# Graph network with skip LSTMs: the LSTM input read in dense runs, the end state transposed in fp32

## The chip, the cores and the metric

The kernel runs on one core of a Trainium2 chip. The metric is the device time of one execution in microseconds (us), the median of repeated runs; lower is better.

## The reference

Eight batch elements of 1,024 nodes with 128 features pass through two graph networks, each followed by a residual sum and a layernorm. The second network ends in four LSTMs over windows of consecutive nodes, one for each window length p = 1, 2, 3, 4; each replaces the last node of its windows, and the next p reads the result. Cut to what matters here:

```python
def _lstm_last(Wih, Whh, bih, bhh, xs):            # xs [windows, p, 128]
    def step(carry, x_t):
        h, c = carry
        g = x_t @ Wih.T + h @ Whh.T + bias
        i, f, gg, o = jnp.split(g, 4, axis=-1)
        c = jax.nn.sigmoid(f) * c + jax.nn.sigmoid(i) * jnp.tanh(gg)
        h = jax.nn.sigmoid(o) * jnp.tanh(c)
        return ((h, c), None)
...
h = jax.nn.relu(jnp.einsum('ts,bsh->bth', adj, x @ Wg0 + bg0))
h = jax.nn.relu(jnp.einsum('ts,bsh->bth', adj, h @ Wg1 + bg1))
for p in range(1, MAX_SKIP + 1):
    nw = Tv // p
    wins = h[:, :nw * p, :].reshape(Bv * nw, p, Hd)
    last = _lstm_last(Wih[p - 1], Whh[p - 1], bih[p - 1], bhh[p - 1], wins)
    idx = jnp.arange(nw) * p + (p - 1)
    h = h.at[:, idx, :].set(last.reshape(Bv, nw, Hd))
...
x = _layernorm(x + _L0_gnn_ref(x, adj, adj, ...), axis=-1)
x = _layernorm(x + _L1_gnn_ref(x, adj, ...), axis=-1)
```

## The kernel before

Everything stays in SBUF, features or nodes on the 128 partitions. Each fp32 product is made of three matmuls of rounded parts (fp32r): high by high, high by low, low by high. `product` issues the three, and its lines L464, L465 and L466 carry nearly all matmuls. ScalarE rounds a result to its high part, VectorE subtracts for the low part (`lo_part`, L916), and only then can the next product read it.

The first network runs in four pairs of batch elements and ends near 547 us. Then come nine slots (0 to 8). A slot works on several batch elements at once: the graph products of element n (`adj_x`, `wg0`, `adj_h`, `wg1`), the LSTM of p = 1 and 2 for element n-1 and of p = 3 and 4 for element n-2. The text calls a window length "span p". Slots 3 to 6 are two turns of a loop over two slots. The orders are written out by hand in the lists `SLOT` (slots 0 to 6), `DRAIN` (slot 7) and `LAST` (slot 8), and all engines follow the same list. An item `step(stream, p, s, ...)` is step s of span p. Spans 1 and 2 run in stream Y, 3 and 4 in X, and element 7 in Z. `("ahead",)` lets TensorE do the input products of the following step early. `held=True` lets the end of a step on ScalarE and VectorE come after the next step's gates. `("fin", v, back)` brings the end state back to nodes on partitions, four tiles of 128 nodes for each v, and adds it to `xb`; `stats`, `root` and `scale` are the layernorm on VectorE.

A step has 3 gates (s = 0) or 4. The gates' input products come first, 3 matmuls for each gate; at s > 0 as many recurrent products on `hstep` follow. That makes, for one batch element, 9 + 12 = 21 input matmuls for span 2, 33 for span 3 and 45 for span 4. After the gates ScalarE applies the functions (L861), VectorE multiplies (L1167 to L1174), ScalarE takes tanh (L871), and VectorE multiplies once more (L1186), casts the high part (L1188) and subtracts the low part (L916).

The state of an element lies in `ht`, features on partitions, nodes in their order along the free axis, in a high and a low part, two elements in turn (`ht_last` for element 7). The input of step s of span p is every p-th column:

```python
first = u.w0 * u.p + u.s
return slice(first, first + u.p * (nw - 1) + 1, u.p)
```

So TensorE's moving operand has a step of 2, 3 or 4 fp32 elements, and the last step of a span writes its state back with that step. `fin` multiplies `ht`, high and low, by an identity: 8 fp32r matmuls for each v (L754, L755), 16 for each element.

Of the kernel before, what the change touches and what calls it, by code (L numbers as in the profile page):

```python
# [8 lines left out]
F32 = mybir.dt.float32  # L29
# [5 lines left out]
P = 128  # L35
# [7 lines left out]
GI, GF, GG, GO = range(4)  # L43


def build(nc, x, adj_t, w1, w2, w3, wg0, bg0, wg1, bg1, wih_t, whh_t, bih, bhh, out):
# [10 lines left out]
    with ctx:  # L57
# [19 lines left out]
        xb = sb("xb", [P, B, MT, F], F32)  # L77
# [14 lines left out]
        HTW = N + 2  # L92
# [9 lines left out]

        ht = sb("ht", [P, 2, 2, HTW], F32R, r3_at)
        gates_at = (r3_at + 4 * 4 * HTW + 63) // 64 * 64
        gates = sb("gates", [P, 2, 5, BANK], F32, gates_at)
        hstep = sb("hstep", [P, 2, 2, BANK], F32R, gates_at + 4 * 10 * BANK)

        ht_last = sb("ht_last", [P, 2, HTW], F32R, adj_at)
        gates_last = sb("gates_last", [P, 5, BANK], F32, adj_at + 12 * KB)
        hstep_last = sb("hstep_last", [P, 2, BANK], F32R, adj_at + 12 * KB + 4 * 5 * BANK)  # L110
        assert gates_at + 4 * 14 * BANK <= lw_raw_at + 4 * (2 * SKIPS - 1) * G4 + 64
# [10 lines left out]
        ident = sb("ident", [P, P], F32R)  # L122
# [44 lines left out]
        h_done = sem("h_done")  # L167
        fin_mm = sem("fin_mm")
# [48 lines left out]
        Step = namedtuple("Step", "stream p s w0 nw n back held")  # L217
        X, Y, Z = 0, 1, 2

        def step(stream, p, s, w0=0, back=None, nw=None, held=False):  # L220
            nw = nw or min(N // p, BANK)
            return Step(stream, p, s, w0, nw, nw + nw % 2, (2 if stream == X else 1) if back is None else back,
                        held)
# [85 lines left out]
        CELL_STEPS = (2, 4)  # L309
# [6 lines left out]
            "cell": lambda n: sum(CELL_STEPS[u.s > 0] for u in steps_of(n)),  # L316
# [9 lines left out]
        FIN_PRE = 2  # L326
# [44 lines left out]
        def span(u, n=None):  # L371

            at = u.w0 % BANK
            return slice(at, at + (n or u.n))

        def h_in(slot, back):

            return ht_last if slot - back == B - 1 else ht[:, :, (slot - back) % 2, :]

        def gates_in(stream):  # L380
            return gates_last if stream == Z else gates[:, stream]

        def hstep_in(stream):
            return hstep_last if stream == Z else hstep[:, :, stream]
# [7 lines left out]
        def columns(u, nw):  # L392

            first = u.w0 * u.p + u.s
            return slice(first, first + u.p * (nw - 1) + 1, u.p)
# [905 lines left out]
```

## Time and profile before

| what | value |
|---|---|
| time, median of 3 runs (lowest, highest) | 1154.91 us (1154.67, 1155.43) |
| the profiled execution's own time, beside its span | span 1154.9 us, which is its time from the first to the last instruction |
| TensorE busy | 1121.8 us (97%) |
| VectorE busy | 583.2 us (50%) |
| ScalarE busy | 386.3 us (33%) |
| GpSimd busy | 0.7 us |
| mean granted TensorE clock | 0.989 of full |

TensorE's busy time counts from a matmul's start to the end of its drain, and matmuls overlap. A matmul's price in a stream is the distance from its start to the start of the next one; its own duration is longer.

### The profile page before, as it was taken

What the parts mean: (1) busy time and instruction counts of PE and PEld (TensorE: products, weight loads), DVE (VectorE), ACT (ScalarE), POOL (GpSimd) and SP (SyncE); (2) the same over time, 40 slices, a digit from 0 to 9 for tenths busy, and PEclk for the clock granted to TensorE, in tenths of its full rate; (3) what the DMA queues carried; (4) which work ended last, traced back from release to release, by engine and by line L of the source; (5) the groups of instructions that cost most, each with busy time, mean ns of one, the idle gap of its engine ahead of it and who ended that gap; (6) DMA issues with size and microseconds to landing.
All of it is one profiled execution on the core that took longest, in us unless ns stands there. A gap on an engine that the chain in (4) does not pass through costs nothing.

```text
span 1154.9 us, 15131 instructions
## 1 busy us (share of the span) xinstructions
PE 1121.8 (97%) x5688; PEld 937.5 (81%) x5688; DVE 583.2 (50%) x1426; ACT 386.3 (33%) x696; POOL 0.7 (0%) x6
## 2 busy tenths in 40 slices
PE   6999999999999999999999999999999999999994
PEld 4888988899888988888776878878788787778694
DVE  7233364243442264247646545565655646565667
ACT  6222012120222012133424443444434443435442
POOL 0000000000000000000000000000000000000000
PEclk9999999999999999999999999999999999999997
DMA  9200000000000000012000000000000000000001
GB/s 312 85 1 1 1 1 1 1 1 1 0 0 0 0 0 0 0 39 106 1 1 1 1 1 1 1 19 1 19 1 0 18 0 2 17 19 1 1 19 37
DMA packets 21744, 20.43 MB, mean 18 GB/s; under 512 B 960, under 2 KB 18496, under 8 KB 21696
## 3 DMA queue, kind: packets, MB, share of 16 engines
q1 hardware_dynamic: 21696, 19.81, 5.4%
q8 instruction: 28, 0.46, 0.2%
q14 instruction: 20, 0.16, 0.0%
HBM read 15.61 MB, written 4.19 MB: 17 GB/s over the span
## 4 chain that ended last, share of the span: by engine, by line
PE 94%; DVE 3%; ACT 1%; DMA 0%; issue 0%; ACTq 0%; SPq 0%; DVEq 0%
PE ps L464 27%; PE ps L465 27%; PE ps L466 27%; PE ps L584 8%; PE ps L563 4%; PE ps L566 1%; DVE adj L916 1%; PE ps L755 1%; PE ps L754 0%; DMA xb<-in_x 0%; PE ps L600 0%; DVE square L982 0%; DVE stats L933 0%; DVE node L916 0%; DVE xb L974 0%
## 5 line engine op out<-in xcount | busy, mean ns | idle before, releaser
L861 ACT ACTIVATE gates<-ps,lb 128x256 f32<-128x256 f32 (+2 forms) x273 | 142.6, 567 | 168.1 <-PE ps L466 155.1
L464 PE MATMUL ps<-adj,node 128*128 128x512 f32 x384 | 151.9, 396 | 12.8 <-DVE adj L916 10.1
L465 PE MATMUL ps<-adj,node 128*128 128x512 f32 x384 | 150.3, 391 | 0.0
L466 PE MATMUL ps<-adj,node 128*128 128x512 f32 x384 | 150.3, 391 | 0.0
L801 ACT ACTIVATE y<-ps 128x512 fp32r<-128x512 f32 x48 | 28.7, 598 | 294.5 <-PE ps L466 294.4
L916 DVE TENSOR_TENSOR y<-ps,y 128x512 fp32r<-128x512 f32 x48 | 33.1, 691 | 186.0 <-ACT y L801 186.0
L466 PE MATMUL ps<-ht,lw 128*128 128x256 f32 (+2 forms) x231 | 112.1, 485 | 0.0
L465 PE MATMUL ps<-ht,lw 128*128 128x256 f32 (+2 forms) x231 | 111.9, 485 | 0.0
L464 PE MATMUL ps<-ht,lw 128*128 128x256 f32 (+2 forms) x231 | 111.0, 480 | 0.0
L464 PE MATMUL ps<-adj,h 128*128 128x512 f32 x256 | 99.7, 389 | 0.0
L465 PE MATMUL ps<-adj,h 128*128 128x512 f32 x256 | 99.7, 389 | 0.0
L466 PE MATMUL ps<-adj,h 128*128 128x512 f32 x256 | 99.6, 389 | 0.0
L464 PEld LDWEIGHTS ps<-adj,node 128*128 128x128 f32 x384 | 73.0, 190 | 28.7 <-DVE adj L916 10.8
L919 DVE SCALAR_TENSOR_TENSOR h<-ps,h 128x512 fp32r<-128x512 f32 x112 | 76.5, 690 | 35.2 <-ACT h L801 34.4
L584 PE MATMUL ps<-s,adj 128*128 128x256 f32 x768 | 93.0, 283 | 0.0
L584 PEld LDWEIGHTS ps<-s,adj 128*128 128x128 f32 x768 | 92.4, 192 | 0.0
L466 PEld LDWEIGHTS ps<-adj,node 128*128 128x128 f32 x384 | 72.5, 189 | 15.7
L465 PEld LDWEIGHTS ps<-adj,node 128*128 128x128 f32 x384 | 72.9, 190 | 14.7
L801 ACT ACTIVATE h<-ps 128x512 fp32r<-128x512 f32 x96 | 57.4, 598 | 48.9 <-PE ps L466 46.1
L466 PEld LDWEIGHTS ps<-ht,lw 128*128 128x128 f32 x231 | 48.0, 208 | 22.2 <-issue 12.2
L1186 DVE TENSOR_TENSOR gates<-gates 128x256 f32<-128x256 f32 (+3 forms) x77 | 42.0, 546 | 39.7 <-ACT gates L871 39.7
L464 PEld LDWEIGHTS ps<-ht,lw 128*128 128x128 f32 x231 | 46.9, 203 | 18.3 <-issue 7.7
(167 smaller groups left out, 1975.5 us busy)
## 6 DMA issues: line engine op xcount, KB each, us to landing
square<-in_adj_t SPq DMA_DIRECT2D x8, 512.0 KB, 8.0
xb<-in_x SPq DMA_DIRECT2D x8, 512.0 KB, 7.5
adj_raw<-in_adj_t SPq DMA_DIRECT2D x8, 512.0 KB, 7.7
out<-xb SPq DMA_DIRECT2D x7, 512.0 KB, 3.2
lw_raw<-in_wih_t SPq DMA_DIRECT2D x1, 1024.0 KB, 5.8
lw_raw<-in_whh_t SPq DMA_DIRECT2D x1, 768.0 KB, 7.3
w_raw<-in_w SPq DMA_DIRECT2D x1, 512.0 KB, 11.0
out<-xb SPq DMA_DIRECT2D x2, 256.0 KB, 2.5
```

Of the source, the lines that this page charges most:

```text
L464: pe.matmul(dst, stat(HI), mov(HI), start=start, stop=False)
L465: pe.matmul(dst, stat(HI), mov(LO), start=False, stop=False)
L466: return pe.matmul(dst, stat(LO), mov(HI), start=False, stop=stop)
L563: pe.matmul(ps[:, q % BANKS, 2 * t * F:(2 * t + 2) * F], h2[:, HI, k, nt:nt + P], w3s[:, k, :, :].rearrange("p a c -> p (a c)"), start=(k ...
L566: last = pe.matmul(ps[:, q % BANKS, 2 * t * F:(2 * t + 1) * F], h2[:, LO, k, nt:nt + P], w3s[:, k, HI, :], start=False, stop=(k == K3 - 1) ...
L584: last = pe.matmul(dst, adj[:, a, m, nt:nt + P], s3[:, b, m, :, :].rearrange("p j c -> p (j c)"), start=(m == 0 and t == 0 and (a, b) == ( ...
L755: last = pe.matmul(dst, h_in(slot, back)[:, LO, nt:nt + P], ident[:], start=False, stop=True)
L801: nc.scalar.activation(dst, ps[:, (j * A_MM + q) % BANKS, :], func).then_inc(a_hi, 1)
L861: nc.scalar.activation(gates_in(u.stream)[:, g, at], ps[:, (AHEAD["gate"][slot] + gate) % GB, 0:u.n], ACT.Tanh if g == GG else ACT.Sigmoid ...
L916: nc.vector.tensor_tensor(dst, src, f32(hi), ALU.subtract).then_inc(done, 1)
L919: nc.vector.scalar_tensor_tensor(out=dst, in0=src, scalar=0.0, in1=f32(hi), op0=ALU.max, op1=ALU.subtract).then_inc(done, 1)
L1186: nc.vector.tensor_tensor(h, h, in_place(v, GG, n), ALU.mult).then_inc(cell_step, 1)
```

## The change

The nodes are put in another order outside the kernel: node i goes to place (i % 4) * 256 + i // 4, four groups of 256 (x, and both sides of the adjacency matrix; the output is put back). In that order the input of span 2 is two runs of 256 adjacent columns. For spans 3 and 4 the state is kept a second time, in `hw`: twelve runs of 86 columns, run r holding the nodes with i % 12 = r, at a pitch of 88. Span 3 reads 4 runs for a step (344 columns where there were 342), span 4 reads 3 (258 where there were 256).

The even runs (the nodes that p = 2 leaves as they are) are copied from `ht` by GpSimd, one copy for the high and one for the low part of each element, after p = 1 and after step 2 of span 4 of the element before. The odd runs are written by VectorE as the end of span 2, and span 3 writes its four runs. The end state of span 3 is summed (high + low) to plain fp32 in `hfull` for three of the four groups; the last step of span 4 writes the fourth group there in one multiply, without a high and a low part. `fin` takes 4 fp32 transposes for each v out of `hfull` instead of 8 fp32r matmuls. `ht` has one buffer instead of two, the streams' `gates` and `hstep` are separate tensors, and the lists of items stay as they are.

```diff
+def node_order(n):
+    return np.arange(n).reshape(n // BLOCKS, BLOCKS).T.reshape(n)
...
+        def inputs_of(u, slot, i):
+            if u.p == 1:
+                return h0[:, i, u.w0:u.w0 + u.n]
+            if u.p == 2:
+                return h_in(slot, u.back)[:, i, :].rearrange("q (w s u) -> q s w u", w=2, s=2)[:, u.s]
+            return runs_in(slot, u.back)[:, i, :].rearrange("q (w s v) -> q s w v", s=u.p, v=PITCH)[:, u.s, :, 0:RUN]
...
+            back = 1
+            for slot in range(back, SLOTS):
+                steps = steps_of(slot)
+                ready = max(k for k, u in enumerate(steps) if u.p == 1 and u.back == back)
+                if slot - back < B - 2:
+                    ready = max([ready] + [k for k, u in enumerate(steps) if (u.p, u.s) == (4, 2)])
+                if slot - back == B - 2:
+                    pool.wait_ge(out_done, 16 * OUT_BEFORE_LATE)
+                pool.wait_ge(h_done, AHEAD["unit"][slot] + ready + 1)
+                of, to = h_in(slot, back), runs_in(slot, back)
+                for i in (HI, LO):
+                    last = nc.gpsimd.tensor_copy(half_of_runs(to[:, i, :], 0), f32(spread(of, i * N, [[N // 2, 2]])))
+                last.then_inc(runs_set, 1)
...
+                        if (u.p, u.s) == (3, 0):
+                            pe.wait_ge(runs_set, batch_of(slot, turn, u.back) + 1)
...
                         for t in range(4):
-                            nt = (4 * v + t) * P
-                            dst = mm_unit(v)[:, t * F:(t + 1) * F]
-                            pe.matmul(dst, h_in(slot, back)[:, HI, nt:nt + P], ident[:], start=True, stop=False)
-                            last = pe.matmul(dst, h_in(slot, back)[:, LO, nt:nt + P], ident[:],
-                                             start=False, stop=True)
+                            at = (2 * v + t // 2) * OPEN_BLOCK + t % 2 * P
+                            last = pe.transpose(mm_unit(v)[:, t * F:(t + 1) * F], full_in(slot, back)[:, at:at + P],
+                                                ident_f[:])
...
+                            if ends(v):
+                                block = full_in(slot, v.back)[:, (BLOCKS - 1) * OPEN_BLOCK:]
+                                nc.vector.tensor_tensor(
+                                    block.rearrange("q (v a) -> q a v", a=PER_BLOCK),
+                                    h.rearrange("q (a v) -> q a v", a=PER_BLOCK),
+                                    tanh.rearrange("q (a v) -> q a v", a=PER_BLOCK), ALU.mult).then_inc(h_done, 1)
+                                continue
...
+                            if (v.p, v.s) == (3, 2):
+                                dve.wait_ge(h_done, ahead("unit", slot, turn, n_ended))
+                                hi, lo = (f32(runs_in(slot, v.back)[:, i, :]).rearrange(
+                                    "q (a b v) -> q b a v", a=PER_BLOCK, v=PITCH)[:, 0:BLOCKS - 1, :, 0:RUN]
+                                    for i in (HI, LO))
+                                nc.vector.tensor_tensor(full_in(slot, v.back)[:].rearrange(
+                                    "q (b v a) -> q b a v", b=BLOCKS, a=PER_BLOCK)[:, 0:BLOCKS - 1], hi, lo, ALU.add)
```

On VectorE, in the second half of a slot, these rows of before stand between the last step of span 4 (`gates`, 256 wide, the first row) and the layernorm's `scale` (the last row); the 512-wide rows are step 0 of span 2:

```order
560 L1186 TENSOR_TENSOR gates<-gates 128x256
561 L1153 REGISTER_ALU
562 L1188 CAST ht<-gates 128x256
563 L1153 REGISTER_ALU
564 L916 TENSOR_TENSOR ht<-gates,ht 128x256
565 L1184 REGISTER_ALU
566 L1186 TENSOR_TENSOR gates<-gates 128x512
567 L1153 REGISTER_ALU
568 L1188 CAST hstep<-gates 128x512
569 L1153 REGISTER_ALU
570 L916 TENSOR_TENSOR hstep<-gates,hstep 128x512
```

In the change the same place reads (`gates_x` is stream X's, `hfull` the fp32 end state):

```order
559 L1224 TENSOR_TENSOR hfull<-gates_x 128x3x86
560 L1218 REGISTER_ALU
561 L1229 TENSOR_TENSOR gates<-gates 128x512
562 L1194 REGISTER_ALU
563 L1246 CAST hstep<-gates 128x512
564 L1194 REGISTER_ALU
565 L966 TENSOR_TENSOR hstep<-gates,hstep 128x512
```

Two instructions of the end of span 4 are gone. At the end of span 3 VectorE has one more in the change, behind the cast and the low part, and ahead of the low part of `z`:

```order
471 L1229 TENSOR_TENSOR gates_x<-gates_x 128x344
472 L1194 REGISTER_ALU
473 L1246 CAST hw<-gates_x 128x4x86
474 L1194 REGISTER_ALU
475 L966 TENSOR_TENSOR hw<-gates_x,hw 128x4x86
476 L1256 TENSOR_TENSOR hfull<-hw 128x3x3x86
477 L1186 REGISTER_ALU
478 L966 TENSOR_TENSOR z<-ps,z 128x512
```

The row with `hfull<-hw` (774 columns) is the added one. GpSimd had only its constants and the identity; now it has two copies for each of the eight elements:

```order
6 L492 MEMSET ident_f 128x128
7 L494 ISA
8 L494 AFFINE_SELECT ident_f<-ident_f 128x128
9 L508 CAST hw<-ht 128x2x3x86 x12
10 L508 CAST hw_late<-ht 128x2x3x86 x2
11 L508 CAST hw_last<-ht_last 128x2x3x86 x2
```

The last three rows are new, 516 columns each.

## Rows read from the trace of the kernel before

**Rows 1.** The page: busy time, the 40 slices, and one costly group.
```profile
PE 1121.8 (97%) x5688; PEld 937.5 (81%) x5688; DVE 583.2 (50%) x1426; ACT 386.3 (33%) x696; POOL 0.7 (0%) x6
...
PE   6999999999999999999999999999999999999994
...
L464 PE MATMUL ps<-ht,lw 128*128 128x256 f32 (+2 forms) x231 | 111.0, 480 | 0.0
```

**Rows 2.** Busy by window: about one slot of the loop (us and count per engine).
```profile
698.00:771.00 73.00, 73.00 (x334) 58.08 (x333) 42.76 (x108) 31.09 (x59) 0.00 (x0) 1.00 0.03 8
```

**Rows 3.** Timeline of TensorE, slot 5: first matmul of each block (start, us).
```profile
698.89 0.46 PE L464 MATMUL ps<-ht,lw 128*128 128x342 f32 x1
701.60 0.43 PE L464 MATMUL ps<-adj,node 128*128 128x512 f32 x1
...
710.69 0.34 PE L464 MATMUL ps<-hstep,lw 128*128 128x342 f32 x1
...
712.60 0.22 PE L464 MATMUL ps<-wgs,z 128*128 128x128 f32 x1
...
745.28 0.39 PE L464 MATMUL ps<-ht,lw 128*128 128x256 f32 x1
...
748.06 0.30 PE L464 MATMUL ps<-hstep,lw 128*128 128x256 f32 x1
...
749.49 0.61 PE L464 MATMUL ps<-ht,lw 128*128 128x512 f32 x1
...
753.59 0.42 PE L464 MATMUL ps<-z,wgs 128*128 128x512 f32 x1
...
754.55 0.61 PE L464 MATMUL ps<-ht,lw 128*128 128x512 f32 x1
...
760.00 0.24 PE L754 MATMUL ps<-ident,ht 128*128 128x128 f32 x1
...
760.87 0.45 PE L464 MATMUL ps<-hstep,lw 128*128 128x512 f32 x1
...
763.69 0.22 PE L754 MATMUL ps<-ident,ht 128*128 128x128 f32 x1
...
772.07 0.46 PE L464 MATMUL ps<-ht,lw 128*128 128x342 f32 x1
```

**Rows 4.** Timeline of VectorE, slot 5: a dense and a stepped cast, two ends.
```profile
745.17 0.29 DVE L1188 CAST hstep<-gates 128x256 fp32r<-128x256 f32 x1
...
755.30 0.40 DVE L1188 CAST ht<-gates 128x256 fp32r<-128x256 f32 x1
...
757.44 0.69 DVE L916 TENSOR_TENSOR hstep<-gates,hstep 128x512 fp32r<-128x512 f32 x1
```

**Rows 5.** Lines of GpSimd: mean ns after the busy us.
```profile
L456 POOL TENSOR_SCALAR_AFFINE_SELECT ident_f<-ident_f 128x128 f32<-128x128 f32 x1 | 0.3, 294 | 0.1
L454 POOL MEMSET ident_f<- 128x128 f32 x1 | 0.2, 205 | 0.3 <-POOLq L1291 0.3
```

**Rows 6.** Timeline of VectorE in slot 1, behind step 0 of span 2.
```profile
612.27 4.19 DVE L974 TENSOR_SCALAR xb<-xb,mv,newton 128x128 f32<-128x128 f32 x16
616.38 0.68 DVE L919 SCALAR_TENSOR_TENSOR h<-ps,h 128x512 fp32r<-128x512 f32 x1
```

**Rows 7.** Timeline of TensorE, slot 8: its start and two waits.
```profile
1049.79 0.39 PE L464 MATMUL ps<-h,lw 128*128 128x512 f32 x1
...
1090.99 0.55 PE L464 MATMUL ps<-ht_last,lw 128*128 128x342 f32 x1 [2.15 <-DVE ht_last L916]
...
1136.23 0.49 PE L464 MATMUL ps<-hstep_last,lw 128*128 128x256 f32 x1 [1.65 <-DVE hstep_last L916]
```

**Rows 8.** Busy by window, with granted clock (the 1.00 or 0.57).
```profile
1091.00:1099.00 8.00, 8.00 (x29) 7.73 (x30) 5.98 (x23) 2.02 (x4) 0.00 (x0) 0.57 0.00 0
```

**Rows 9.** Timeline of VectorE: the end of the last step of all.
```profile
1140.79 0.39 DVE L1188 CAST ht_last<-gates_last 128x256 fp32r<-128x256 f32 x1
1141.22 0.61 DVE L916 TENSOR_TENSOR ht_last<-gates_last,ht_last 128x256 fp32r<-128x256 f32 x1
```

More of the change, by code:

```diff
@@ L307, in count, with ends, cell_steps @@
             return sum(item[0] == name for item in items(slot) if not isinstance(item, Step))
-        CELL_STEPS = (2, 4)
+        def ends(u):
+            return u.p == SKIPS and u.s == SKIPS - 1
+        def cell_steps(u):
+            return (2 if u.s > 0 else 0) + (0 if ends(u) else 2)
         PER_SLOT = {
@@ L369, in needs, with span, runs_in, full_in @@
             return before(slot, k, lambda v, b: b + v.back == u.back and (v.p, v.s) == (u.p - 1, u.p - 2))
-        def span(u, n=None):
-            at = u.w0 % BANK
-            return slice(at, at + (n or u.n))
+        def span(u):
+            return slice(0, u.n)
         def h_in(slot, back):
-            return ht_last if slot - back == B - 1 else ht[:, :, (slot - back) % 2, :]
+            return ht_last if slot - back == B - 1 else ht
+        def runs_in(slot, back):
+            return hw_last if slot - back == B - 1 else hw_late if slot - back == B - 2 else hw
+        def full_in(slot, back):
+            return hfull_last if slot - back == B - 1 else hfull_late if slot - back == B - 2 else hfull
         def gates_in(stream):
-            return gates_last if stream == Z else gates[:, stream]
+            return (gates_x, gates, gates_last)[stream]
         def hstep_in(stream):
-            return hstep_last if stream == Z else hstep[:, :, stream]
+            return (hstep_x, hstep, hstep_last)[stream]
         def place_before(slot, k):
@@ L616, in bank_free @@
                         pe.wait_ge(a_lo, A_PRE + PAIRS * A_LO_PAIR)
-                    elif slot >= 2:
-                        pe.wait_ge(fin_add, ahead("fin", slot, turn, FIN_PRE + r - 1))
+                    elif slot >= 3:
+                        pe.wait_ge(fin_add, ahead("fin", slot, turn, r - 1))
                 def mm_unit(r):
@@ L1245, in dve_slot @@
                         if item[0] == "stats":
-                            dve.wait_ge(fin_add, ahead("fin", slot, turn, FIN_PRE + n_fin))
+                            dve.wait_ge(fin_add, ahead("fin", slot, turn, n_fin))
                             group_stats(groups, at)
@@ L1250, in dve_slot @@
                             v = item[1]
-                            dve.wait_ge(fin_add, ahead("fin", slot, turn, FIN_PRE + n_fin))
+                            dve.wait_ge(fin_add, ahead("fin", slot, turn, n_fin))
                             last = row_stats(groups[4 * v:4 * v + 4])
```

129 lines of the change are left out of this document (77 added, 52 removed).

## The prediction

> **What bounds the kernel now.** I read the page first: TensorE is busy for 97% of the span, and its row of tenths shows 9 in nearly every slice; VectorE has 50%, ScalarE 33%, GpSimd nothing [rows 1]. Then the windows: in 73 us of the loop TensorE is busy all the time at full clock, VectorE for 42.8 us and ScalarE for 31.1 [rows 2]. Busy time alone doesn't prove a full TensorE, since matmuls overlap, so the third view is the timeline, where the distance from one block to the next is what a block costs [rows 3]. A slot of the loop is 772.07 - 698.89 = 73.18 us. The reader should compare four pairs there. 9 input products of span 2 take 753.59 - 749.49 = 4.10 us and 12 take 5.45, so 0.455 each; 12 recurrent products of the same 512 columns, from dense `hstep`, take 763.69 - 760.87 = 2.82, so 0.235. For span 3, 9 input products take 2.71, 0.301 each, and 12 dense ones of 342 columns take 1.91, 0.159 each. For span 4, 12 take 2.78, 0.232 each, and 12 dense ones 1.43, 0.119 each. Same engine, clock and width; only the step of the moving operand differs, and a step of 2, 3 or 4 elements costs the same factor, 1.9 to 2. TensorE bounds the loop, and 99 matmuls of each element (231 x 3 plus those on `ht_last`, 792 in all [rows 1]) are read at half rate.
>
> **What each part is worth.** Input products, for one element:
> - span 2: 21 x (0.455 - 0.232) = 4.7 us. I take 0.232 for a dense one; 0.235 is the row, and stationary loads alike.
> - span 3: 33 x (0.301 - 0.160) = 4.65 us. The 2 extra columns of 344 are in the 0.160.
> - span 4: 45 x (0.232 - 0.120) = 5.0 us.
>
> Together 14.4 us, if runs of 86 and 256 columns are read like one dense stretch. The trace has no moving operand in several runs. The bounds are the dense rows (14.4) and the stepped rows for spans 3 and 4 (4.7 only). I take the dense ones: 85 of 86 steps inside a run are steps to the neighbour.
>
> `fin`: 8 matmuls of 128 columns take 760.87 - 760.00 = 0.87 us, 0.109 each, 1.7 us for an element [rows 3]. The change has 8 fp32 transposes instead of 16. No row has one. Below, it costs what one fp32r matmul costs, 0.109, and an element gains 0.85 us. Above, full fp32 is done as four passes of parts: 0.44 each, 3.5 us, a loss of 1.8. I take the lower end, since a transpose multiplies nothing and the kernel's own three-part product exists for the sake of multiplying.
>
> The Trainium skill speaks on both sides: "TensorE: Matmul & The Clock Gate", Terms, says that the transpose mode is four times faster for fp32, and "FP8 and Floating Point Precision", TensorE Precision Notes, that true fp32 takes four passes. No row here decides it.
>
> VectorE: the end of span 4 loses a cast and a low part, 0.40 and some 0.6 us; span 3 gains an addition of 774 columns, about 1.0 us by 0.69 for 512 [rows 4]. Even in sum. The stepped cast took 0.40 where a dense one of the same size took 0.29, so the stepped reads at the end of span 2 may add up to 0.5 us for an element. All of that lies under TensorE in the loop, and costs its full length where TensorE waits for a state.
>
> GpSimd: two copies of 516 columns for each element. Its only rows of size are 128 columns in 0.205 and 0.294 us [rows 5], which scale to 0.83 and 1.19; with the 40% that a step cost VectorE up to 1.7. So 1.7 to 3.4 us for both. They may start when step 2 of span 4 is done, some 2 us before span 2 starts, and are needed at the next slot's span 3, some 18 us after it even in the shortened slot. Hidden, if only TensorE waits for them.
>
> **Slot by slot.** Shortening TensorE makes the chains behind it count. From the end of step 0 of span 2 to its state on VectorE takes 758.13 - 753.59 = 4.5 us [rows 3, 4]; between lie `wg1` (0.96), 12 input products (2.8 instead of 5.45) and one `fin` (0.9, or 0.45). So it is just covered, by some tenths; the same count leaves 0.7 to 1.3 us at the recurrent products of spans 3 and 4. No stall, but little room.
> - Slot 1 has only span 2: 4.7. But there VectorE follows that state with 4.19 us of scaling and 0.68 of a low part that the next slot's first gates need [rows 6]. 4.5 + 4.9 = 9.4 us at most, against 0.96 + 2.8 + 2.8 = 6.6 of TensorE; I take 2.0 us of new waiting. Gain 2.7.
> - Slots 2 to 6: 5 x (14.4 + 0.85) = 76.3.
> - Slot 7 has 21 products of span 2, 42 of span 3, 21 of span 4 and no `fin`: 4.7 + 5.9 + 2.35 = 13.0. It interleaves two elements and graph products; full.
> - Slot 8 has 21, 57 and 114, and two `fin` before its end: 4.7 + 8.0 + 12.8 + 1.7 = 27.2 out of the 86.4 us from 1049.79 to 1136.23 [rows 7]. TensorE already waits there, 2.15 us for the last state of span 2 and 1.65 for the last of span 4. An input block of 1.4 to 1.9 us covers less of a chain of 2.7 to 4.5 us than one of 2.8 to 3.6. Going through `LAST` item by item I get new waits of 0.3 to 2.3 us ahead of eight later blocks, 7.1 in sum. The wait of 2.15 grows to about 3, and behind it the granted clock was 0.57 [rows 8]; there the 21 first input products of span 3 lose their gain, about 2.4 us after what VectorE hides. The very end gains 1.07 us: a cast (0.39) and a low part (0.61) that TensorE and VectorE waited for are gone [rows 9]. 27.2 - 7.1 - 2.4 + 1.1 = 18.8.
>
> Sum: 2.7 + 76.3 + 13.0 + 18.8 = 110.8. The profiled span is 1154.9, the median 1154.91, so the two need no correction: **1044 us**.
>
> **Rivals.**
> - The loop stalls. GpSimd's copies run just while VectorE ends span 4 and starts span 2. If one holds the other off, up to 3.4 us of delay fall on a chain with tenths of room: about 3 us for each of six slots, 1062 us. For it: VectorE's 42.8 us must fit in 58 instead of 73. Against it: with the short copy (1.7) the gaps of VectorE take it.
> - The transposes take four passes: 2.65 us more for each of seven elements (the eighth lies under VectorE's scaling), 1062 or 1063 us.
> - Runs are not read densely: spans 3 and 4 keep their price, 8 x 9.65 = 77 us less, somewhat made up by the waits that then don't arise: 1118 us. For it only that no row has such an operand.
> - A step of 2 costs nothing as such, and span 2 was slow for another reason. Then 38 us of the gain fall away, 1080 us. What speaks against it is the pair 0.455 and 0.235 in the same slot on the same width [rows 3]; that the two differ in their stationary operand is all that is left for it.
> - Slower than before: GpSimd's copies are so slow that span 3 waits in every slot. The chain from step 2 of span 4 to span 3 has about 20 us of room; the gain of 15.3 a slot would be gone when both copies take 35 us, 34 ns a column. At 20 us a copy it would be some 1180 us. The rows give 1.6 to 2.3 ns a column, so this needs a factor of 15.
>
> The last but one of these is the Trainium skill's: "SBUF — State Buffer", SBUF: two separate sides, says that SBUF has lines of 16 bytes, that two hits in a line suffice for full bandwidth, and so that up to 4 fp32 can be stepped for free. By that rule span 2 would gain nothing. The trace disagrees with it: a step of 2 costs as much as one of 4.
>
> "GPSIMD Engine Reference", Performance pitfalls for Q7 kernels, gives about 2.9 cycles an element for reads with a step over 8 bytes, at 1.2 GHz; an estimate by that page is 1.25 us a copy, inside my bounds, and nothing changes.
>
> **How the numbers follow.** Forecast (1034 to 1054) 61 in 100; loop stalls 17; four passes 12; runs not dense 4; a free step of 2, 3; slower 3. The first three cover the range: 1034, where slot 8 loses half as much and the clock holds, to 1066, either of the two rivals at its full price. A measurement of this kernel tells 0.2% (2.3 us) from no change. Faster: 96; the same: 1; slower: 3.
>
> **What would show it.** Right: input products of 512, 344 and 258 columns at 0.23, 0.16 and 0.12 us from start to start; a slot of the loop at 58 us with TensorE busy throughout; VectorE's idle time before gates much smaller; transposes 0.11 apart; GpSimd's copies 1 to 1.7 us each; new waits of TensorE in slot 1 and all over slot 8, the largest ahead of element 7's first span 3. Wrong: gaps of TensorE in the loop ahead of the recurrent products of spans 2 to 4 or ahead of `adj_h`, VectorE instructions that last longer while GpSimd copies, transposes 0.2 us or more apart, or a granted clock below full for longer than before in the last slot (0.57 over 8 us is some 6.9 us at half).

## The result and the profile after

The changed kernel takes 1044.87 us (median of 4 runs, 1043.99 to 1046.42), the kernel before 1155.08 beside it; the ratio is 0.9046, with a 95% interval of 0.9034 to 0.9059. The profiled execution took 1043.99 us, with a span of 1042.1. Operations stand at new lines (and move by a few in the experiments): L516 to L518 are the three products, L805 the transposes, L508 GpSimd's copies, L966 a low part.

The page answers to [rows 1]:
```profile
PE 1001.4 (96%) x5624; PEld 881.9 (85%) x5624; DVE 584.9 (56%) x1415; ACT 379.2 (36%) x696; POOL 19.8 (2%) x22
...
PE   5999999999999999999998999999999999999883
```
TensorE lost 120 us of busy time and is still what bounds the kernel; it is below 9 in the first slice, in one in the middle (8) and in the last three (8, 8, 3). VectorE's busy time is nearly the same as before, in a shorter span. One slot of the loop, by window, beside [rows 2]:
```profile
737.73:795.73 58.00, 58.00 (x327) 51.53 (x326) 42.79 (x106) 29.57 (x58) 2.73 (x2) 1.00 0.03 10
```
The slot takes 58.00 us instead of 73.18, with TensorE busy for all of it at full clock, and GpSimd for 2.73. TensorE's timeline of slot 5, with the first matmul of each block (start, us), answers to [rows 3]:
```profile
775.87 0.28 PE L516 MATMUL ps<-hw,lw 128*128 128x258 f32 x1
...
777.35 0.28 PE L516 MATMUL ps<-hstep_x,lw 128*128 128x258 f32 x1
...
778.79 0.40 PE L516 MATMUL ps<-ht,lw 128*128 128x512 f32 x1
...
780.88 0.39 PE L516 MATMUL ps<-z,wgs 128*128 128x512 f32 x1
...
784.56 0.60 PE L805 MATMUL ps<-ident_f,hfull 128*128 128x128 f32 x4
784.92 0.48 PE L516 MATMUL ps<-hstep,lw 128*128 128x512 f32 x1
...
795.73 0.32 PE L516 MATMUL ps<-hw,lw 128*128 128x344 f32 x1
...
797.16 0.39 PE L516 MATMUL ps<-adj,node 128*128 128x512 f32 x1
```
12 products of span 4 take 777.35 - 775.87 = 1.48 us, 0.123 each (0.232 before); 9 of span 2 take 2.09, 0.232 each (0.455); 9 of span 3 take 1.43, 0.159 each (0.301). The reader is to look at distances: the durations of single matmuls overlap.

VectorE's state of step 0 of span 2 is what the products at 784.92 need. The first row is of the kernel before, the other two of the changed kernel:
```profile
755.73 0.61 DVE L916 TENSOR_TENSOR ht<-gates,ht 128x256 fp32r<-128x256 f32 x1
```
```profile
782.10 0.51 DVE L1224 TENSOR_TENSOR hfull<-gates_x 128x258 f32<-128x258 f32 x1 [0.30 <-ACT gates_x L921]
...
783.82 0.69 DVE L966 TENSOR_TENSOR hstep<-gates,hstep 128x512 fp32r<-128x512 f32 x1
```
Before, the cast of span 4 and this low part (0.40 and 0.61 us) stood ahead of the end of step 0, and the state came 758.13 - 753.59 = 4.54 us after TensorE's gates. In the changed kernel they are gone, and it comes 784.51 - 780.88 = 3.63 us after them.

Slot 1 and the last slot hold TensorE's new waits, in the brackets at the ends of the rows; they answer to [rows 7]:
```profile
609.36 0.51 PE L516 MATMUL ps<-hstep,lw 128*128 128x512 f32 x1
...
614.06 0.50 PE L516 MATMUL ps<-h,lw 128*128 128x512 f32 x1 [1.65 <-DVE h L969]
...
987.14 0.65 PE L516 MATMUL ps<-hw_last,lw 128*128 128x344 f32 x1 [3.06 <-DVE hw_last L966]
...
1005.06 0.39 PE L516 MATMUL ps<-hstep,lw 128*128 128x258 f32 x1 [1.22 <-DVE hstep L966]
...
1024.42 0.58 PE L516 MATMUL ps<-hstep_last,lw 128*128 128x258 f32 x1 [3.18 <-DVE hstep_last L966]
...
1029.21 1.09 PE L805 MATMUL ps<-ident_f,hfull_last 128*128 128x128 f32 x8 [1.84 <-DVE hfull_last L1224]
```
The largest waits are 3.18 us, 1.5 more than in the same place before, and 3.06, 0.9 more. Where the 112.8 us between the two spans lie, from the starts of the same blocks in both timelines:

| stretch | before | after | gain | predicted |
|---|---|---|---|---|
| up to the first `h` gates of slot 1 | 596.54 | 595.04 | 1.5 | 0 |
| slot 1, from the `ht` gates to the next `h` gates | 13.28 | 10.61 | 2.7 | 2.7 |
| slots 2 to 6 | 365.8 | 290.1 | 75.7 | 76.3 |
| slot 7 | 65.76 | 52.73 | 13.0 | 13.0 |
| slot 8 to the end | 105.1 | 85.2 | 19.9 | 18.8 |

GpSimd's timeline, and VectorE's beside two of its copies:
```profile
776.59 2.73 POOL L508 CAST hw<-ht 128x516 fp32r<-128x516 f32 x2 [55.29 <-DVE hstep_x L966]
...
919.44 1.68 POOL L508 CAST hw_late<-ht 128x516 fp32r<-128x516 f32 x2 [24.10 <-DVE ht L966]
969.48 2.06 POOL L508 CAST hw_last<-ht_last 128x516 fp32r<-128x516 f32 x2 [48.36 <-DVE ht_last L966]
```
```profile
777.04 1.53 DVE L966 TENSOR_TENSOR node<-xb,node 128x1024 fp32r<-128x1024 f32 x1
...
969.67 1.11 DVE L1212 TENSOR_TENSOR gates_x<-gates_x 128x258 f32<-128x258 f32 x1
970.81 1.01 DVE L1215 TENSOR_TENSOR gates_x<-gates_x 128x258 f32<-128x258 f32 x1
```
Two copies take 1.68 us where VectorE leaves GpSimd alone and 2.73 where it works; `node` takes 1.53 instead of the 1.22 of before, and instructions of 0.42 us on VectorE take 1.0 to 1.1 beside a copy. The two engines do hold each other off. Not every instruction is slowed: the low part of `h`, which reads `ps`, starts at 778.49 in the middle of a copy and takes its 0.68 us. No wait of TensorE in the loop comes of it; the experiments ask how near it is to one.

### The profile page after: what moved, and what is told of

Same layout as the page of the kernel before. It is cut to its first block, busy times and chain, and to the rows that moved or that the text cites. A ratio compares the mean times of both kernels' runs of the same rounds, so it can differ in the third digit from the quotient of the medians.

```text
span 1042.1 us, 15018 instructions
## 1 busy us (share of the span) xinstructions
PE 1001.4 (96%) x5624; PEld 881.9 (85%) x5624; DVE 584.9 (56%) x1415; ACT 379.2 (36%) x696; POOL 19.8 (2%) x22
## 4 chain that ended last, share of the span: by engine, by line
PE 88%; DVE 8%; ACT 2%; issue 1%; DMA 0%; ACTq 0%; SPq 0%; DVEq 0%
PE ps L516 25%; PE ps L517 24%; PE ps L518 24%; PE ps L636 9%; PE ps L615 4%; PE ps L618 1%; DVE adj L966 1%; DVE xb L1024 1%; ACT gates_last L911 1%; PE ps L805 0%; DMA xb<-in_x 0%; DVE gates_last L1229 0%; DVE node L966 0%; PE ps L652 0%; DVE square L1032 0%
## 5 line engine op out<-in xcount | busy, mean ns | idle before, releaser
L516 PE MATMUL ps<-adj,node 128*128 128x512 f32 x384 | 151.6, 395 | 12.7 <-DVE adj L966 10.0
L518 PE MATMUL ps<-adj,node 128*128 128x512 f32 x384 | 150.4, 392 | 0.0
L966 DVE TENSOR_TENSOR y<-ps,y 128x512 fp32r<-128x512 f32 x48 | 33.1, 691 | 186.0 <-ACT y L851 186.0
L516 PE MATMUL ps<-adj,h 128*128 128x512 f32 x256 | 99.7, 389 | 0.0
L518 PE MATMUL ps<-adj,h 128*128 128x512 f32 x256 | 99.6, 389 | 0.0
L516 PEld LDWEIGHTS ps<-adj,node 128*128 128x128 f32 x384 | 72.6, 189 | 28.0 <-DVE adj L966 10.7
L911 ACT ACTIVATE gates<-ps,lb 128x512 f32<-128x512 f32 (+2 forms) x117 | 70.7, 649 | 43.4 <-PE ps L518 29.3
L518 PEld LDWEIGHTS ps<-adj,node 128*128 128x128 f32 x384 | 72.5, 189 | 15.5
L911 ACT ACTIVATE gates_x<-ps,lb 128x258 f32<-128x258 f32 (+1 forms) x156 | 67.2, 508 | 34.4 <-PE ps L518 34.4
L615 PE MATMUL ps<-w3s,h 128*128 128x256 f32 x256 | 59.6, 333 | 0.0
L618 PE MATMUL ps<-w3s,h 128*128 128x128 f32 x256 | 56.9, 222 | 0.0
L518 PEld LDWEIGHTS ps<-adj,h 128*128 128x128 f32 x256 | 48.1, 188 | 10.1
L516 PEld LDWEIGHTS ps<-adj,h 128*128 128x128 f32 x256 | 48.1, 188 | 9.8
L517 PEld LDWEIGHTS ps<-adj,h 128*128 128x128 f32 x256 | 48.1, 188 | 9.7
```

Of the source, the lines that this page charges most:

```text
L516: pe.matmul(dst, stat(HI), mov(HI), start=start, stop=False)
L517: pe.matmul(dst, stat(HI), mov(LO), start=False, stop=False)
L518: return pe.matmul(dst, stat(LO), mov(HI), start=False, stop=stop)
L615: pe.matmul(ps[:, q % BANKS, 2 * t * F:(2 * t + 2) * F], h2[:, HI, k, nt:nt + P], w3s[:, k, :, :].rearrange("p a c -> p (a c)"), start=(k ...
L618: last = pe.matmul(ps[:, q % BANKS, 2 * t * F:(2 * t + 1) * F], h2[:, LO, k, nt:nt + P], w3s[:, k, HI, :], start=False, stop=(k == K3 - 1) ...
L911: nc.scalar.activation(gates_in(u.stream)[:, g, at], ps[:, (AHEAD["gate"][slot] + gate) % GB, 0:u.n], ACT.Tanh if g == GG else ACT.Sigmoid ...
```

## Experiments: what a run must have to be read at full rate

Ratios are to the kernel before, run beside the experiment on the same chip; 0.001 of it is 1.16 us. The changed kernel itself stands at 0.9046.

**The step, span 2 alone.** In `inputs_of`:
```diff
-                return h_in(slot, u.back)[:, i, :].rearrange("q (w s u) -> q s w u", w=2, s=2)[:, u.s]
+                return h_in(slot, u.back)[:, i, u.s:u.s + 2 * (u.n - 1) + 1:2]
```


> The changed kernel, but the 21 input products of span 2 of each element read `ht` with a step of 2 again, as the kernel before did (they read even and odd columns, so other values enter the states of span 2; everything else stays). If the step is what made them slow: 512-column products 0.455 us from start to start instead of 0.232, 4.7 us more in each of slots 2 to 7, about 3 in slot 1, where the 1.65 us wait ahead of the `h` gates goes first, and 3 to 4 in slot 8: 1078 to 1081 us. If a step of 2 is free as such (the rival of the prediction) and something else of the old kernel, its padded `ht` for instance, made span 2 slow: 0.23 us from start to start and 1045 us.

Measured: 1080.37 us, ratio 0.9346 (0.933 to 0.9361). TensorE's timeline, the first matmul of the block of 9 and of the block behind it:
```profile
728.20 0.61 PE L516 MATMUL ps<-ht,lw 128*128 128x512 f32 x1
...
732.24 0.41 PE L516 MATMUL ps<-z,wgs 128*128 128x512 f32 x1
```
9 in 4.04 us, 0.449 each. The same operand, place and stationary tensor as at 0.232, only the step is back; that settles that the step is the cost in span 2. The wait of 1.65 us in slot 1 is gone, as expected.

**The step, spans 3 and 4.** With `PITCH` 86 as well, and GpSimd's copy waiting for step (4, 3) instead of (4, 2):
```diff
-            return runs_in(slot, u.back)[:, i, :].rearrange("q (w s v) -> q s w v", s=u.p, v=PITCH)[:, u.s, :, 0:RUN]
+            return runs_in(slot, u.back)[:, i, u.s:u.s + u.p * (u.n - 1) + 1:u.p]
```


> The changed kernel, but the input products of spans 3 and 4 read columns s, s + p, s + 2p, ... of the same 1032 columns of `hw`, with the runs end to end (`PITCH` 86), and GpSimd's copy waits for the last step of span 4 (other values enter spans 3 and 4, the counts of columns stay). If the step is the cost: 344 columns at 0.30 and 258 at 0.235 us from start to start, 9.65 us for each element less what slot 8 then waits less, 70 to 77 us: 1113 to 1122 us. If the runs gained nothing by density but by something else, for instance by GpSimd's copy into a second tensor, the pitches stay at 0.16 and 0.12 and the time at 1045 us.

Measured: 1120.07 us, ratio 0.9685 (0.9669 to 0.9701). TensorE's timeline has 12 products of 344 columns in 703.92 - 700.28 = 3.64 us, 0.303 each, and 12 of 258 columns in 2.79 us, 0.232 each. The step is the cost in spans 3 and 4 as well:
```profile
700.28 0.47 PE L516 MATMUL ps<-hw,lw 128*128 128x344 f32 x1
...
703.92 0.36 PE L516 MATMUL ps<-hstep_x,lw 128*128 128x344 f32 x1
...
749.81 0.50 PE L516 MATMUL ps<-hstep,lw 128*128 128x512 f32 x1 [0.52 <-DVE hstep L966]
```
The last row was not expected: in every slot of the loop TensorE waits 0.52 us for the state of span 2's step 0. VectorE's timeline ahead of it:
```profile
747.49 0.98 DVE L1246 CAST hstep<-gates 128x512 fp32r<-128x512 f32 x1
748.50 1.26 DVE L966 TENSOR_TENSOR hstep<-gates,hstep 128x512 fp32r<-128x512 f32 x1
```
These two took 0.43 and 0.69 us in the changed kernel. Here GpSimd's copy starts later, at 746.81, and so lies beside them. That is the stall of the prediction's first rival, made by moving the copy by one step. It makes 2.6 of the 74 us that this kernel is slower; the rest isn't the stall.

**Runs of 2 and 4 columns.** Span 2 reads pairs in step 0 and fours in step 1, each beginning on a multiple of 4 columns:
```diff
+                run = (2, 4)[u.s]
+                return h_in(slot, u.back)[:, i, :].rearrange("q (w g v) -> q w g v", g=2, v=run)[:, :, 0]
```


> The changed kernel, but step 0 of span 2 reads `ht` in pairs (2 columns, 2 left out) and step 1 in fours (4 columns, 4 left out); other columns enter span 2, their count of 512 stays. Three theories of what a run must have. (a) Only the share of steps to the neighbour counts, each jump costs one more column: pairs 1.5 times 0.232, so 0.34 us, fours 1.25 times, 0.29 us; 9 x 0.11 + 12 x 0.06 = 1.7 us an element, 1056 to 1059 us. (b) Short runs are as dense as long ones from 2 columns on: 0.232 for both, 1045 us. (c) Anything short of a long run is read like a step: 0.455 for both, 1078 to 1081 us.

Measured: 1060.77 us, ratio 0.9177 (0.9162 to 0.9193). None of the three theories holds for both steps: TensorE's timeline gives the 9 products in pairs 730.07 - 726.03 = 4.04 us, 0.449 each, as slow as a step, and the 12 in fours 733.82 - 731.02 = 2.80, 0.233 each, as fast as a dense stretch.
```profile
726.03 0.61 PE L517 MATMUL ps<-ht,lw 128*128 128x512 f32 x1
...
730.07 0.41 PE L517 MATMUL ps<-z,wgs 128*128 128x512 f32 x1
...
731.02 0.39 PE L517 MATMUL ps<-ht,lw 128*128 128x512 f32 x1
...
733.82 0.60 PE L806 MATMUL ps<-ident_f,hfull 128*128 128x128 f32 x4
```
So what matters is either a run of 4, or that the whole of 4 columns on a 16-byte boundary is read. The next two kernels tell these apart.

**Runs off the 16-byte grid.** `RUN, PITCH = 86, 86`: every second long run begins two columns off.

> The changed kernel with its runs end to end (86 columns from start to start of a run instead of 88), so that only every second run starts where the pitch of 88 lets all start, on a multiple of 16 bytes; same computation. If the start of a run doesn't matter: 0.160 and 0.120 us from start to start for 344 and 258 columns, 1045 us within 1. If runs that start off that grid are read slower: pitches up to 0.23 and 0.18 at most (half of the runs at the stepped price), up to 39 us more, 1084 us.

Measured: 1045.99 us, ratio 0.9043 (0.9028 to 0.9058), the changed kernel's. The timeline has 12 products of 258 columns in 722.94 - 721.50 = 1.44 us, 0.120 each. Where a long run starts doesn't matter, so the padding to 88 columns buys nothing here.

**Fours and eights off the grid.**
```diff
+                if u.s == 0:
+                    return h_in(slot, u.back)[:, i, :].rearrange("q (w v) -> q w v", v=8)[:, :, 2:6]
+                return h_in(slot, u.back)[:, i, :].rearrange("q (w v) -> q w v", v=16)[:, :, 1:9]
```


> The changed kernel, but step 0 of span 2 reads fours of columns that begin two columns behind a multiple of four (so each four reaches over a 16-byte boundary) and step 1 reads eights that begin one column behind such a multiple; other columns enter span 2, 512 each. In the run before, fours that begin on the multiple went at 0.233 us and pairs at 0.451. Theory 1, the run's length decides, from 4 columns on: both 0.232 us from start to start, 1045 us. Theory 2, a column is cheap only where its whole group of 16 bytes is read: the fours have none (0.451), the eights have one of 4 columns and 4 single ones (0.34): 9 x 0.22 + 12 x 0.11 = 3.3 us an element, 1068 to 1071 us.

Measured: 1067.73 us, ratio 0.9229 (0.9215 to 0.9244). TensorE's timeline:
```profile
727.08 0.61 PE L518 MATMUL ps<-ht,lw 128*128 128x512 f32 x1
...
731.12 0.41 PE L518 MATMUL ps<-z,wgs 128*128 128x512 f32 x1
...
732.08 0.49 PE L518 MATMUL ps<-ht,lw 128*128 128x512 f32 x1
...
735.99 0.60 PE L807 MATMUL ps<-ident_f,hfull 128*128 128x128 f32 x4
```
The fours, 9 in 4.04 us, are at 0.449: a run of 4 over a boundary is worth nothing. The eights, 12 in 3.91 us, are at 0.326. Theory 2 had 0.451 and 0.34. One rule comes near all the operands tried (steps of 2, 3, 4, pairs, fours on and off the grid, eights): a column of 4 bytes costs one unit (0.232 / 512 = 0.45 ns) where the whole aligned group of 4 is read, and two where any of the group is left out. It is a few per cent high for all that aren't dense: it gives 0.464 for the 0.449 of a step of 2 or of pairs, 0.318 for the 0.303 of a step of 3, and 0.348 for the 0.326 of the eights, where it is worst. Eights off the grid leave one group with three columns read, and no run tells what three of four cost. By this rule a long run pays twice only for the columns at its ends. A run of 86 has 21 whole groups and 2 columns over, whether it begins on the grid or two columns off it, so `PITCH` 86 had to come out the same.

The Trainium skill, "SBUF — State Buffer", SBUF: two separate sides, asks for two or more hits in a line of 16 bytes for full bandwidth. The trace disagrees for TensorE's moving operand: pairs have two hits in each line and went at half rate.

## Experiments: the transposes

**Plain fp32 products.** In `fin`:
```diff
-                            last = pe.transpose(mm_unit(v)[:, t * F:(t + 1) * F], full_in(slot, back)[:, at:at + P],
-                                                ident_f[:])
+                            last = pe.matmul(mm_unit(v)[:, t * F:(t + 1) * F], full_in(slot, back)[:, at:at + P],
+                                             ident_f[:], start=True, stop=True)
```


> The changed kernel, but the 8 products of `fin` of each element are plain fp32 products with the identity instead of fp32 transposes, on the same operands; same values. If full fp32 products take four passes and the transposes were cheap because they multiply nothing: 0.44 us from start to start instead of 0.109, 2.65 us more for each of slots 2 to 6, less in slot 8 where waits cover part, 16 to 20 us in sum: 1061 to 1065 us. If an fp32 operand of 128 columns costs 0.109 us in either mode: 1045 us within 1.

Measured: 1049.43 us, ratio 0.9081 (0.9063 to 0.91), 4 us slower than with transposes, not 16 to 20. The timeline:
```profile
727.41 1.05 PE L805 MATMUL ps<-ident_f,hfull 128*128 128x128 f32 x8
728.22 0.48 PE L516 MATMUL ps<-hstep,lw 128*128 128x512 f32 x1
```
The four products of a `fin` stand as eight records and take 0.81 us to the next block, where four transposes stood as four and took 784.92 - 784.56 = 0.36. A slot of the loop takes (857.42 - 739.53) / 2 = 58.95 us by the starts of its span 3, 0.93 more. Both theories fail on the size. A plain fp32 product of 128 columns costs 0.81 / 4 = 0.20 us, two of the 0.109 and not four, and the transpose saves one of the two. The price of four passes had been built on an fp32r product of 128 columns, and that is a poor unit: it costs 0.109 us where its columns at 0.45 ns come to 0.058. Four times 0.058 is 0.23, near the measured 0.2; the number of passes itself isn't shown. The Trainium skill's four passes, "FP8 and Floating Point Precision", TensorE Precision Notes, can be right in this way; the records of this trace show two for each product.

**`fin` as before.** Sixteen fp32r products on `ht`, with `ident` built again:
```diff
-                            last = pe.transpose(mm_unit(v)[:, t * F:(t + 1) * F], full_in(slot, back)[:, at:at + P],
-                                                ident_f[:])
...
+                            pe.matmul(dst, h_in(slot, back)[:, HI, nt:nt + P], ident[:], start=True, stop=False)
+                            last = pe.matmul(dst, h_in(slot, back)[:, LO, nt:nt + P], ident[:],
+                                             start=False, stop=True)
```


> The changed kernel, but `fin` is done as before the change, by 16 fp32r products of 128 columns on the high and low parts in `ht` (which hold the state of span 1, so the outputs are other sums; `hfull` is still written). The transposes' own part of the gain: 8 x 0.109 = 0.87 us an element, for slots 2 to 6 and two or three `fin` in slot 8: 4.4 to 6.5 us more, 1049 to 1051.5 us. If the fewer matmuls were swallowed by waits in the loop: 1045 to 1046 us.

Measured: 1049.98 us, ratio 0.9074 (0.9058 to 0.9091), 3.2 us slower than the changed kernel by the ratios; a slot of the loop takes (859.39 - 741.54) / 2 = 58.93 us, 0.91 more. The transposes' part of the gain is thus 0.91 us a slot, as predicted (0.85).

## Experiments: who copies, and how much

**VectorE copies.** GpSimd's loop is taken out, and behind the end of the same step VectorE does
```diff
+                                for i in (HI, LO):
+                                    last = nc.vector.tensor_copy(
+                                        half_of_runs(runs_in(slot, 1)[:, i, :], 0),
+                                        f32(spread(h_in(slot, 1), i * N, [[N // 2, 2]])))
+                                last.then_inc(runs_set, 1)
```


> The changed kernel, but VectorE makes the two copies of 516 columns instead of GpSimd, right behind its end of step 2 of span 4 (or of span 1 where that comes last); same computation. Two copies of 0.5 to 0.6 us lie on VectorE's queue ahead of the end of step 3 of span 4 and of step 0 of span 2. If the chain behind span 2 has only the tenths of room that the prediction gave it and VectorE goes into it late: 0.5 to 1 us in each of slots 2 to 6, 1048 to 1051 us. If VectorE has idle time ahead of it in the loop that takes the copies, as its idle time before gates says, and GpSimd no longer slows it: 1044 to 1046 us.

Measured: 1045.44 us, ratio 0.9042 (0.9029 to 0.9055), no difference. VectorE's timeline in the same place:
```profile
720.41 0.95 DVE L1250 CAST hw<-ht 128x516 fp32r<-128x516 f32 x2
721.26 0.70 DVE L961 TENSOR_TENSOR z<-ps,z 128x512 fp32r<-128x512 f32 x1
721.86 1.23 DVE L961 TENSOR_TENSOR node<-xb,node 128x1024 fp32r<-128x1024 f32 x1
```
Both copies cost VectorE 0.95 us, and `node` is back from 1.53 to 1.23. VectorE has idle time here and takes the copies; GpSimd was not needed for them.

**Three times the copies.** Each copy waits for the one before it, and a last one of 6 columns says that the runs are set:
```diff
-                for i in (HI, LO):
-                    last = nc.gpsimd.tensor_copy(half_of_runs(to[:, i, :], 0), f32(spread(of, i * N, [[N // 2, 2]])))
-                last.then_inc(runs_set, 1)
+                for again in range(3):
+                    for i in (HI, LO):
+                        last = nc.gpsimd.tensor_copy(half_of_runs(to[:, i, :], 0),
+                                                     f32(spread(of, i * N, [[N // 2, 2]])))
...
+                nc.gpsimd.tensor_copy(half_of_runs(to[:, HI, :], 0)[:, :, :, 0:1],
+                                      f32(spread(of, 0, [[N // 2, 2]]))[:, :, :, 0:1]).then_inc(runs_set, 1)
```


> The changed kernel, but GpSimd makes its two copies of 516 columns three times for each element before it says that the runs are set; same values. It is then at work for some 8 us of each slot of the loop instead of 2.7. If all of that is hidden and VectorE's instructions, which last longer beside it (1.53 instead of 1.22 us in one case), have room: 1045 to 1046.5 us. If GpSimd and VectorE hold each other off on a chain without room (the rival of the prediction): the further 5.5 us of copying make TensorE wait in each slot, 1 to 3 us, 1051 to 1063 us, and gaps of TensorE stand in the loop.

Measured: 1053.32 us, ratio 0.9105 (0.9091 to 0.9119). GpSimd's timeline, then VectorE's beside it, then the wait of TensorE that comes of it in each of the five slots of the loop (0.71 to 0.76 us):
```profile
721.47 7.12 POOL L510 CAST hw<-ht 128x516 fp32r<-128x516 f32 x6 [51.49 <-DVE hstep_x L973]
```
```profile
724.41 1.11 DVE L1219 TENSOR_TENSOR gates_x<-gates_x 128x258 f32<-128x258 f32 x1
725.55 1.00 DVE L1222 TENSOR_TENSOR gates_x<-gates_x 128x258 f32<-128x258 f32 x1
726.48 1.37 DVE L1215 TENSOR_TENSOR gates<-gates 128x512 f32<-128x512 f32 x1
727.76 1.21 DVE L1231 TENSOR_TENSOR hfull<-gates_x 128x258 f32<-128x258 f32 x1
```
```profile
730.76 0.50 PE L523 MATMUL ps<-hstep,lw 128*128 128x512 f32 x1 [0.72 <-DVE hstep L973]
```
The rival's mechanism is real: four instructions of 0.42 to 0.69 us take 1.00 to 1.37, the state of step 0 comes late, and the recurrent products of span 2 wait. It takes three times the copying to make 1.0 us of a slot, (859.60 - 741.58) / 2 = 59.01. Slot 8 has two further waits here, 1.73 us for `hstep_x` and 0.49 for `hstep_last`. In the changed kernel the low part of that state ends at 784.51 and the products start at 784.92: 0.4 us of room.

## Experiments: the new waits

**The scaling behind `h`.** In `items`:
```diff
-                if slot == 1 and isinstance(item, Step) and item[:3] == (Y, 2, 0):
+                if slot == 1 and item == ("wg1", 1):
```


> The changed kernel, but in slot 1 VectorE scales the pairs (16 instructions, 4.2 us) behind the low part of `h` on which the next slot's gates wait, instead of ahead of it; same computation. If that scaling is what TensorE's new wait of slot 1 consists of: the 1.65 us ahead of the `h` gates shrink to a few tenths, 1.3 to 1.7 us less, 1043 to 1043.7 us (ratio to before down by 0.001 to 0.0015). If the low part was late anyway because of its own chain, the wait stays: 1045 us. The price to fear: the end of span 2 of element 0 comes later instead and the next slot's span 3 waits.

Measured: 1043.32 us (1041.55 to 1046.27), ratio 0.9015 (0.9003 to 0.9027). TensorE's timeline in slot 1:
```profile
612.87 0.50 PE L516 MATMUL ps<-hstep,lw 128*128 128x512 f32 x1
...
615.76 0.39 PE L516 MATMUL ps<-h,lw 128*128 128x512 f32 x1
```
The wait is gone: 2.89 us between the two blocks instead of 4.70. From there to GpSimd's copy of slot 7 the kernel takes 921.00 - 612.87 = 308.13 us, the changed kernel 919.44 - 609.36 = 310.08; the 1.95 us are kept. The median's gain against the changed kernel, 3.6 us by the ratios, is more than that and holds scatter. Its profiled execution, at 1046.27, was the slowest of its five; one reason for such scatter is in the section on the hardware.

**The scaling, and two steps of the last slot swapped.** In `LAST`, besides:
```diff
-                step(X, 4, 3, back=3), step(Z, 2, 1, held=True), step(Y, 4, 0, back=2), ("fin", 0, 3),
-                ("ahead",), step(Z, 3, 0), ("fin", 1, 3), ("ahead",), ("stats", 3),
+                step(Y, 4, 0, back=2), step(Z, 2, 1, held=True), step(X, 4, 3, back=3),
+                ("ahead",), step(Z, 3, 0), ("fin", 0, 3), ("fin", 1, 3), ("ahead",), ("stats", 3),
```


> The scaling moved as in the run beside this one, and in the last slot element 5's last step of span 4 stands behind element 7's last step of span 2, where element 6's first step of span 4 stood, and the two change places, with both `fin` behind the first products of span 3; same computation. The block behind the awaited state then has 24 products of 258 columns (2.9 us) instead of 18 and 4 transposes (2.5), with one `fin` more later: the wait of 3.06 us shrinks by 0.4 to 1 us if the chain of 4.6 us is all it consists of, and the two changes together give 1.7 to 2.7 us: 1042 to 1043.3 us. If VectorE, busy with element 5's end on the same queue, is late instead: no gain or a loss of up to 1 us against moving the scaling alone.

Measured: 1045.73 us, ratio 0.9043 (0.903 to 0.9055): the swap costs what the scaling gave. TensorE's timeline has a wait that neither theory named, and the old one a little longer:
```profile
976.13 0.39 PE L516 MATMUL ps<-hw_late,lw 128*128 128x258 f32 x1 [2.64 <-DVE hw_late L966]
...
989.27 0.66 PE L516 MATMUL ps<-hw_last,lw 128*128 128x344 f32 x1 [3.29 <-DVE hw_last L966]
```
Element 6's first step of span 4 reads the last state of its span 3, and that was just being made; element 5's step had covered its chain. From GpSimd's copy to element 7's span 3 it is 989.27 - 919.07 = 70.20 us, 67.70 in the changed kernel.

**The scaling, and one `fin` ahead.**
```diff
-                step(X, 4, 3, back=3), step(Z, 2, 1, held=True), step(Y, 4, 0, back=2), ("fin", 0, 3),
-                ("ahead",), step(Z, 3, 0), ("fin", 1, 3), ("ahead",), ("stats", 3),
+                step(X, 4, 3, back=3), step(Z, 2, 1, held=True), step(Y, 4, 0, back=2), ("fin", 0, 3), ("fin", 1, 3),
+                ("ahead",), step(Z, 3, 0), ("ahead",), ("stats", 3),
```


> The scaling moved as in `scale_later`, and in the last slot the second `fin` of element 5 stands ahead of the awaited first products of span 3 instead of behind them (element order otherwise as in the changed kernel); same computation. Its 4 transposes took 0.77 us behind those products, where the granted clock was at its lower level; in the wait they are free. If the wait is set by VectorE's chain alone it shrinks from 3.05 to 2.6 us and what follows begins 0.4 to 0.8 us earlier: ratio to before 0.901 to 0.903, 1042 to 1043.5 us. If the transposes' evacuation by VectorE, which now stands ahead of its end of span 2, makes that later by its 0.68 us: no gain against `scale_later`.

Measured: 1043.35 us, ratio 0.9027 (0.9011 to 0.9044). The wait is 2.61 us instead of 3.06, but span 3 starts no earlier: 987.24 - 919.54 = 67.70 us, as before. The wait was VectorE's chain, so filling it moved only the idle time. The last recurrent block starts 1023.92 - 987.24 = 36.68 us behind it instead of 37.28. Against `scale_later` the intervals overlap; both are the fastest versions found, and the scaling is the part that is shown.

## Why the prediction held

- **The step is the cost, long runs are dense**: right, shown by putting the step back for span 2, and for spans 3 and 4 together. Two rivals fall with it: that a step of 2 is free, and that several runs aren't read like one.
- **14.4 and 0.85 us an element**: slots 2 to 6 gave 15.1 us each instead of 15.25; putting the parts back costs 0.0300 of the time (35 us) for span 2, 0.0639 (74, of which 2.6 are the new wait) for spans 3 and 4, and 0.91 us a slot for `fin`.
- **GpSimd hidden**: right. The step "if only TensorE waits for them" was too small a worry: the two engines slow each other by a factor of 1.2 to 2.6, and only the place of the copies, beside instructions that nobody waits for, and 0.4 us of room keep it out of the time. VectorE's instructions that last longer beside a copy were listed as a sign of being wrong; they came without the stall. The bounds for both copies (1.7 to 3.4) held, 1.68 to 2.73; of single ones (1 to 1.7) they did not, 0.86 to 1.91.
- **"Just covered, by some tenths"**: the loop didn't stall, but not by this count, and in part by luck. With the 0.45 that the prediction itself put down for a `fin` of transposes, 0.96 + 2.8 + 0.45 = 4.2 us of products stood against a chain of 4.5: 0.3 short. The chain of 4.5 was read from a trace in which a cast and a low part of span 4 (0.40 and 0.61) lie ahead of it on VectorE. The prediction counts these two as gone, but not out of this chain. Measured, the chain is 3.63 and the cover 784.92 - 780.88 = 4.04, and that is where the 0.4 us of room come from.
- **Slot 1**: the new wait was sized 2.0, where its own terms gave 9.4 - 6.6 = 2.8 at most, and is 1.65; moving the scaling away removed it.
- **Slot 8**: the new waits ahead of the last `fin` were sized 7.1. The waits of this slot are 3.06, 0.56, 1.22, 1.09, 0.16, 0.19 and 3.18, together 9.5, against 3.8 before: 5.7 new. The wait said to grow "to about 3" is 3.06, and the one ahead of the last `fin` fell from 2.82 to 1.84, 0.98 for the predicted 1.07. 27.2 - 5.7 + 1.0 is 22.5 and 19.9 were gained. The 2.6 between them come near the 2.4 put down for the clock, by luck. The clock took about half: of the 21 first products of span 3 the nine behind the wait take 2.75 us at a granted clock of 0.50 (2.81 before) and lose their 1.3, but the twelve behind the `fin` start at 990.41 at 1.00 again and take 2.18 (3.74 before), nearly their full gain. The rest is small and spread: the recurrent blocks of the slot take 0.8 us more in sum than before, and several blocks now end in a wait, which shows the end of their last product too. The new wait said to be the largest, ahead of element 7's first span 3, grew by 0.9 us; the one ahead of the last recurrent products grew by 1.5, to 3.18.
- **Four passes**: unlikely, rightly, but priced at 0.44 us for a product that costs 0.20 (2.65 us a slot, where 0.93 was measured).
- **"The two need no correction"** failed, without harm to the sum. In the later runs the time is mostly 1.7 to 1.9 us above the span, and the spans differ by 112.8 us where 110.8 were summed; 1.5 of the 2.0 is a stretch at the lower clock that the profile before has and the profile after hasn't, below; that is luck, not the change. The medians differ by 1155.08 - 1044.87 = 110.2.

## What to carry over

Read the moving operand's cost as distance from start to start and compare it with a dense block of the same width in the same slot; where fp32 columns are stepped or in pairs, copying them into runs of whole aligned fours halves the matmul, and an otherwise idle engine can do it. Count a chain with the instructions that the change leaves on it, and its cover with those that the change puts there: here one of the two was taken from before, and the count came out on the right side by luck. When two engines slow each other, ask which instructions the work lies beside: the same two copies cost nothing in one place and 0.52 us a slot one step later. A wait on a chain isn't shortened by filling it; and a step moved to cover one wait uncovers another.

## What the runs showed of the hardware

The rate of TensorE's moving operand in fp32 goes by aligned groups of 16 bytes, not by the length of a run. For 512 columns: 0.232 us dense, 0.233 in aligned fours, 0.449 in pairs, in fours over a boundary and with a step of 2, 0.326 in eights that begin one column off. No pattern tried cost more than twice the dense one.

The price of a stepped operand hardly depends on the granted clock. In the kernel before, twelve products of 342 columns with a step of 3 take 1099.12 - 1095.38 = 3.74 us, 0.312 each, in a window at 0.54, and such products take 0.300 to 0.305 at 1.00. Dense runs of 344 columns take 0.305 at 0.50 and 0.162 at 1.00 in the changed kernel. So at the lower level of 1.2 GHz the change gains nothing on these products.

The lower clock isn't in the same places in all executions. Two windows behind the same wait of 1.5 us, of `scale_later` and then of the changed kernel, whose programs are the same up to there. The granted clock is 0.56 in the one, nearly all of it at the lower level of 1.2 GHz, and 1.00, the level of 2.4, in the other:
```profile
574.70:578.60 3.90, 3.90 (x10) 3.09 (x11) 3.86 (x29) 1.83 (x3) 0.00 (x0) 0.56 0.00 0
```
```profile
572.80:576.70 3.90, 3.87 (x17) 3.23 (x18) 3.86 (x29) 2.54 (x4) 0.00 (x0) 1.00 0.00 0
```
The kernel before has such a stretch there as well, 9 products in 3.64 us at 0.56 where the changed kernel takes 2.16, and that is the 1.5 us of the table's first line. A difference of 1 to 2 us between two profiles of this kernel is to be read block by block, not from their spans.
